# Attention scores from a key matrix folded per head, and three value tiles of sixteen in fp32

## The chip, the cores and the metric

The kernel runs on one NeuronCore of a Trainium2 chip, as one launch. Its five engines are TensorE (PE; its weight loads are listed as PEld), VectorE (DVE), ScalarE (ACT), GpSimd (POOL) and SyncE (SP, which here only issues DMAs). The metric is the device time in microseconds (us); lower is better.

## The reference

One transformer block with adaptive layer norm, on x of shape (4, 1024, 256), fp32:

```python
h = layernorm(x) * (1 + ca) + sa
c_q = h @ W_DQ + b_DQ; c_kv = h @ W_DKV + b_DKV            # 32 features each
q_c, k_c, v_c = up-projections of c_q / c_kv, 8 heads x 128
q_r = c_q @ W_QR + b_QR (8 heads x 32); k_r = h @ W_KR + b_KR (32, shared by all heads)
attn = softmax(concat(q_c, q_r) @ concat(k_c, k_r).T / sqrt(160)) @ v_c
x = x + ga * (attn @ W_O + b_O)
h = layernorm(x) * (1 + cb) + sb
x = x + gb * mixture_of_8_experts(h)      # top 1, capacity 768, GELU
```

The change is in the attention: 4 batches x 8 heads = 32 heads, each with a 1024 x 1024 score matrix.

## The kernel before

The program has four stages, each an `nc.Block`. Stage one normalises x, projects it to a key/value latent and a query latent of 32 features each, and folds the weights. Stage two is the attention, from about 86 to 605 us. Stage three projects, normalises again and routes. Stage four runs the experts. No engine crosses a block's end before the others have reached it.

In the attention no head's keys are ever expanded. A score is a product of a *folded query* with the batch's 64 key features (32 latent, 32 rotary), because W_UQ and W_UK are multiplied together in stage one (side product `GQS`, lines 575 and 397 to 409) into `GQ`, 98 rows by 8 heads by 128. fp32 precision is kept by splitting numbers into a high and a low fp16 part; row groups of 32 or 64 partitions hold the parts.

Names: `KA` [128, 4096] holds the key features (rows 0 to 63 high, 64 to 127 low), `KB` [65, 4096] the high part again with a row of -1, `KC` a copy of the high part for the second 512 keys on partitions 64 to 127, `CQ` [98, 4096] the query latents (high, low, high and two rows of 1), `QA` and `QB` a ring of three heads of folded queries, `prob` the exponentials in fp32 (8 tiles of 128 keys by 1024 queries), `prob_top` the upper 16 bits of `prob` read as bf16 in place, `prob_lo` the fp16 remainder, `VV` the values as two 32-column halves and a column of ones.

The order on each engine is written out by hand over slots (p, k), with p a head and k one of its 8 tiles of 128 keys. In slot (p, k):

- PE runs two score halves of tile k + 4 (line 710), each as two accumulating products of 512 queries, `KA` by `QA` (line 722) and `KB` by `QB` (line 723); a row of `QB` holds the query's row maximum, which the row of -1 subtracts. The two halves alternate between the PSUM banks `st_ps`, so each waits until ACT has read the same bank two halves before.
- PE runs `maxima` of head p + 2 (line 725): for 128 queries, two products of 64 rows each with the two halves of the keys (lines 732, 733), into the three banks `x_ps`. DVE reduces each bank to one column (line 859), and after 16 of them reduces those to `mz` (line 866).
- In slots 4 and 6 PE makes half of the folded query of head p + 3 (`query`, line 751) in `side_ps`; ACT copies its high part to `QA` (line 803), DVE subtracts to get the low part in `QB` (line 871). The next half waits for that.
- In slot 1 PE turns `mz` into 8 rows (line 758), ACT copies them (line 809), SP sends them by DMA into row 64 of `QB` (line 704).
- PE runs `values(p, k)` (line 771): 8 groups of 128 queries, each with `prob_top` and `prob_lo` as stationary operand and 65 columns of `VV` as moving one, 16 products in all.
- ACT makes the exponentials of tile k + 4 (line 799), two of 512 columns per slot.
- The subtraction `prob - prob_top` into `prob_lo` is POOL's (line 834), except for tile 5 of every head and tile 7 of odd heads, which `by_vector` gives to DVE (line 876): 6.5 of 8 tiles on POOL, 1.5 on DVE.
- At a head's end ACT copies the accumulators (line 816), DVE adds the halves (line 884) and inverts the sums (line 885), POOL normalises (line 841). `values(p + 1, 0)` waits for the first two.

Of the kernel before, what the change touches and what calls it, by code (L numbers as in the profile page):

```python
# [15 lines left out]
P = 128  # L16
# [22 lines left out]
QRING = 3  # L39


def adaln_block(nc, h_t, W_DQ, b_DQ, W_UQ, b_UQ, W_DKV, b_DKV, W_UK, b_UK, W_UV, b_UV, W_QR, b_QR,
# [20 lines left out]
    with ctx:  # L63
# [44 lines left out]
        KC = sb(inner, "KC", [P, B, HALF], fp16)  # L108
        KB = sb(inner, "KB", [LR + 1, N], fp16)
        CQ = sb(inner, "CQ", [QROWS, N], fp16)  # L110
        VV = sb(inner, "VV", [P, NT, VP], fp16)
        GQ = sb(inner, "GQ", [QROWS, H, P], fp16)
        mz = sb(inner, "mz", [P, ST], fp16)
        mrow = sb(inner, "mrow", [ST, 2, P], fp16)
# [28 lines left out]
        G = sb(one, "G", [QROWS, H, P])  # L143
# [52 lines left out]
        SHIFT, COLUMNS, GATES, UQ, UKV, PROJ, BIAS, GQS, SIDE = 0, 1, 2, 4, 6, 7, 9, 10, 11  # L196
        GATE_STEPS = 5

        with nc.Block() as block:
# [43 lines left out]
            def _(ac):  # L243
# [47 lines left out]
                for b in range(B):  # L291
# [5 lines left out]
                    nc.scalar.activation(KC[LR:P, b, :], k_ps[LR:P, HALF:S], ACT.Identity, bias=bk[LR:P, :]).then_inc(hi_done, 1)  # L297
# [6 lines left out]
                    nc.scalar.activation(CQ[0:3 * DC, b * S:(b + 1) * S], q_ps[0:3 * DC, :], ACT.Identity,  # L304
# [5 lines left out]
            def _(pool):  # L310
# [30 lines left out]
                fill(12, KB[LR:LR + 1, :], -1.0)  # L341
# [3 lines left out]
                fill(13, CQ[3 * DC:QROWS, :], 1.0)  # L345
                pool.wait_ge(const_p, 14)
                for g in range(2, NG):
                    power(g)

            @block.vector  # L350
            def _(v):
# [22 lines left out]
                def side_out(n):  # L374
# [15 lines left out]
                    elif n == UKV:  # L390
                        nc.vector.tensor_copy(ukvT[:], bank[:].rearrange("p (h c) -> p h c", h=H)).then_inc(side_done, 1)
                    elif n < BIAS:
                        nc.vector.tensor_copy(proj[:, n - PROJ, :], bank[:, 0:D]).then_inc(side_done, 1)
                    elif n == BIAS:
                        nc.vector.tensor_copy(attn_bias[:], bank[:, 0:D]).then_inc(side_done, 1)
                    else:
                        g_ps = bank[0:QROWS, 0:H * DC].rearrange("p (h c) -> p h c", h=H)
                        nc.vector.tensor_scalar(G[:, :, 0:DC], g_ps, SCALE, None, ALU.mult).then_inc(prep, 1)
                        nc.vector.tensor_scalar(G[:, :, LR:LR + DC], g_ps, SCALE, None, ALU.mult).then_inc(side_done, 1)
                        for r in range(2):  # L400
                            nc.vector.tensor_scalar(G[:, :, r * LR + DC:(r + 1) * LR], qr[:], SCALE, None, ALU.mult).then_inc(prep, 1)
                        v.wait_ge(prep, 3)
                        v.wait_ge(side_done, GQS + 1)
                        nc.vector.tensor_copy(GQ[:], G[:]).then_inc(prep, 1)
                        v.wait_ge(prep, 4)

                        nc.vector.tensor_tensor(GQ[64:QROWS, :, :], G[64:QROWS, :, :], GQ[64:QROWS, :, :], ALU.subtract).then_inc(prep, 1)
                        v.wait_ge(prep, 5)
                        nc.vector.tensor_copy(GQ[96:97, :, :], G[96:97, :, :]).then_inc(prep, 1)
# [12 lines left out]
                def keys_low(b):  # L422
                    at = slice(b * S, (b + 1) * S)
                    v.wait_ge(hi_done, 3 * b + 2)
                    nc.vector.scalar_tensor_tensor(KA[LR:P, at], k_ps[LR:P, :], bk[LR:P, :], KA[LR:P, at],
                                                   ALU.add, ALU.subtract).then_inc(lo_done, 1)
                    nc.vector.tensor_copy(KB[0:LR, at], KA[0:LR, at])

                def queries_low(b):
                    at = slice(b * S, (b + 1) * S)  # L430
                    v.wait_ge(hi_done, 3 * b + 3)
                    nc.vector.scalar_tensor_tensor(CQ[DC:2 * DC, at], q_ps[DC:2 * DC, :], bq[DC:2 * DC, :],
                                                   CQ[DC:2 * DC, at], ALU.add, ALU.subtract).then_inc(lo_done, 1)

                def take_values(b):
                    v.wait_ge(v_ready, b + 1)
                    for low in range(2):
                        nc.vector.tensor_copy(VV[:, b * ST:(b + 1) * ST, (1 - low) * DC:(2 - low) * DC],
                                              v_ps[:, :, low * LR:low * LR + DC]).then_inc(v_done, 1)

# [58 lines left out]
                side_out(GQS)  # L499
# [9 lines left out]
            def _(te):  # L509
# [30 lines left out]
                def values(b):  # L540
                    te.wait_ge(lo_done, 2 * b + 1)
                    if b:
                        te.wait_ge(v_done, 2 * b)
# [4 lines left out]
                def side(n):  # L548
# [67 lines left out]
                side(GQS)  # L616
                turn(7)
                values(2)
# [9 lines left out]
        QA = sb(two, "QA", [P, QRING, S], fp16)  # L628
        QB = sb(two, "QB", [LR + 1, QRING, S], fp16)
# [15 lines left out]
        sub_vector = sem("sub_vector")  # L645
# [3 lines left out]
        q_ready = sem("q_ready")  # L649
        qa_done = sem("qa_done")  # L650
        ql_done = sem("ql_done")
        max_done = sem("max_done")
        mrow_ready = sem("mrow_ready")
        mrow_done = sem("mrow_done")
# [10 lines left out]
        QUERY_SLOTS = (4, 6)  # L665
        FIRST_MAX = 0
        ROW_SLOT = 1

        def by_vector(n):

            return (5, 7) if n % 2 else (5,)

        def by_pool(n):

            return [k for k in range(ST) if k not in by_vector(n)]

        pool_before = [sum(len(by_pool(m)) for m in range(n)) for n in range(HEADS)]
        vector_before = [sum(len(by_vector(m)) for m in range(n)) for n in range(HEADS)]
# [11 lines left out]
        def maxima_of(p, k):  # L690

            n, s = (p + 2, k - FIRST_MAX) if k >= FIRST_MAX else (p + 1, k - FIRST_MAX + ST)
            return n, (2 * s, 2 * s + 1)

# [4 lines left out]
        with nc.Block() as block:  # L699
            @block.sync  # L700
            def _(sp):
                for n in range(HEADS):
                    sp.wait_ge(mrow_done, n + 1)
                    sp.dma_start(QB[LR:LR + 1, n % QRING, :].rearrange("a (t q) -> a t q", q=P),
                                 mrow[:, n % 2, :]).then_inc(mrow_in[n % 2], 16)

            @block.tensor
            def _(te):
                mm = nc.tensor.matmul

                def scores(n, k, f):
# [4 lines left out]
                    if k == 0:  # L716
                        te.wait_ge(qa_done, 2 * n + f + 1)
                        te.wait_ge(ql_done, 2 * n + f + 1)
                        te.wait_ge(mrow_in[n % 2], 16 * (n // 2 + 1))
                    at = slice(b * S + k * P, b * S + (k + 1) * P)  # L720
                    half = slice(f * HALF, (f + 1) * HALF)
# [3 lines left out]
                def maxima(n, q):  # L725
                    b = n // H
                    i = n * 16 + 2 * q
                    if i >= 2:
                        te.wait_ge(smax_done, i - 1)
                    te.wait_ge(qa_done, 2 * n + q // 4 + 1)  # L730
                    at = slice(q * P, (q + 1) * P)
                    mm(x_ps[i % 3][:], QA[0:LR, n % QRING, at], KA[0:LR, b * S:b * S + HALF], start=True, stop=True)  # L732
                    mm(x_ps[(i + 1) % 3][:], QA[LR:P, n % QRING, at], KC[LR:P, b, :], start=True, stop=True).then_inc(smax_ready, 1)  # L733
# [814 lines left out]
```

## Time and profile before

| | |
|---|---|
| median of 3 runs | 1004.4 us (1001.28 to 1005.44) |
| the profiled execution | 1002.6 us, of which the span is 1000.9 us |
| PE, busy share of the span | 88% |
| VectorE | 71% |
| ScalarE | 59% |
| GpSimd | 66% |
| mean granted TensorE clock | 0.943 of 2.4 GHz |
| attention stage, from its first product to its last normalisation | 86.0 to 604.7 us |

A busy share on PE counts overlapping matmuls as they are displayed, so a PE shown as busy may still be waiting inside; the distance from one start to the next is what a matmul costs. The rows come further below, after the change.

### The profile page before, as it was taken

The numbers are of one execution on the slowest core, as the hardware profiler recorded it, in microseconds if no ns is written. First come the engines' busy times: TensorE is split into PE (matmuls) and PEld (weight loads), VectorE is DVE, ScalarE is ACT, GpSimd is POOL, SyncE is SP. The second block draws the span as 40 slices with busy tenths as digits, with TensorE's granted clock in tenths as the row PEclk, the third lists the DMA queues.
The fourth block names the chain that finished last, engine by engine and source line by source line (L and its number), as shares of the span: only waits on it lengthen the run. The fifth ranks groups of instructions, "written<-read, shape, count | busy, mean of one in ns | idle before, by whom it ended". The sixth has DMA issues, their size and how long they took to land. (4 is left out here: it accounts for less than half of the span.)

```text
span 1000.9 us, 21467 instructions
## 1 busy us (share of the span) xinstructions
PE 881.8 (88%) x8406; PEld 527.7 (53%) x8406; DVE 713.9 (71%) x1315; ACT 588.0 (59%) x1004; POOL 655.7 (66%) x437
## 2 busy tenths in 40 slices
PE   4893899999999999999999988962499999999995
PEld 1350244444444444444444547862266777677764
DVE  4768888888888888888898836872075666566643
ACT  3750577777777777777777663664265446544650
POOL 4200599999999999999999993698404524442452
PEclk9995799999999999999999998985599999999998
DMA  9910000000000000000000004259525434543110
GB/s 279 339 43 0 1 2 2 2 2 2 2 2 2 2 2 2 2 2 2 2 2 1 3 1 169 99 198 320 201 69 162 143 107 140 175 142 123 43 52 19
DMA packets 48166, 71.61 MB, mean 72 GB/s; under 512 B 7508, under 2 KB 40473, under 8 KB 47938
## 3 DMA queue, kind: packets, MB, share of 16 engines
q1 hardware_dynamic: 38114, 53.13, 16.1%
q0 software_dynamic: 7680, 16.87, 5.2%
q8 instruction: 68, 1.11, 0.5%
q10 hardware_dynamic: 2272, 0.24, 0.2%
q14 instruction: 32, 0.26, 0.1%
HBM read 46.76 MB, written 29.67 MB: 76 GB/s over the span
## 5 line engine op out<-in xcount | busy, mean ns | idle before, releaser
L834 POOL TENSOR_TENSOR prob_lo<-prob 128x1024 f16<-128x1024 f32 x208 | 437.3, 2130 | 95.0 <-ACT prob L799 94.9
L799 ACT ACTIVATE prob<-st_ps 128x512 f32<-128x512 f32 x512 | 301.4, 597 | 131.8 <-PE st_ps L723 129.5
L859 DVE TENSOR_REDUCE part_max<-x_ps 128x1 f32<-128x512 f32 x512 | 325.1, 678 | 66.7 <-PE x_ps L733 65.7
L722 PE MATMUL st_ps<-QA,KA 128*128 128x512 f16 x512 | 198.1, 387 | 0.5 <-ACT prob L799 0.5
L723 PE MATMUL st_ps<-QB,KB 65*128 65x512 f16 x512 | 196.4, 384 | 0.0
L771 PE MATMUL acc_ps<-VV,prob 128*128 128x65 f16 x2048 | 159.3, 194 | 3.9 <-POOL prob_lo L834 3.9
L771 PEld LDWEIGHTS acc_ps<-VV,prob 128*128 128x128 bf16 x2048 | 143.6, 98 | 33.4 <-POOL prob_lo L834 6.1
L771 PE MATMUL acc_ps<-VV,prob_lo 128*128 128x65 f16 x2048 | 158.7, 194 | 0.0
L771 PEld LDWEIGHTS acc_ps<-VV,prob_lo 128*128 128x128 f16 x2048 | 134.9, 98 | 29.9
L1340 POOL DMA_INDIRECT out<-yo,xb x48 | 47.7, 993 | 153.3 <-DVE yo L1447 151.1
L732 PE MATMUL x_ps<-KA,QA 64*128 64x512 f16 x256 | 102.2, 399 | 20.8 <-DVE part_max L859 20.7
L1370 ACT ACTIVATE act_f<-g_ps,cols 128x768 f32<-128x768 f32 x64 | 57.6, 900 | 104.3 <-PE g_ps L1493 104.3
L1418 DVE TENSOR_TENSOR act_l<-act_f,act_h 128x768 f16<-128x768 f32 x64 | 59.9, 955 | 71.9 <-ACT act_h L1378 71.9
L1508 PE MATMUL y_ps<-w2h,act_h 128*128 128x256 f16 x384 | 104.8, 273 | 4.2 <-DVE act_l L1418 4.2
L1508 PE MATMUL y_ps<-w2l,act_h 128*128 128x256 f16 x384 | 104.7, 273 | 0.0
L1508 PE MATMUL y_ps<-w2h,act_l 128*128 128x256 f16 x384 | 104.7, 273 | 0.0
L733 PE MATMUL x_ps<-KC,QA 64*128 64x512 f16 x256 | 102.2, 399 | 0.0
L732 PEld LDWEIGHTS x_ps<-KA,QA 64*128 64x128 f16 x256 | 23.8, 93 | 122.6 <-DVE part_max L859 120.5
L722 PEld LDWEIGHTS st_ps<-QA,KA 128*128 128x128 f16 x512 | 49.5, 97 | 60.0 <-issue 36.5
L1333 POOL DMA_INDIRECT tb<-tbuf,xb x48 | 63.9, 1331 | 17.9 <-issue 14.3
L876 DVE TENSOR_TENSOR prob_lo<-prob 128x1024 f16<-128x1024 f32 x48 | 61.2, 1274 | 6.2 <-ACT prob L799 6.2
L1493 PE MATMUL g_ps<-xh,w1h 128*128 128x384 f16 x256 | 53.0, 330 | 1.8 <-DVE xl L1412 1.4
(177 smaller groups left out, 1346.7 us busy)
## 6 DMA issues: line engine op xcount, KB each, us to landing
w1f<-in_L_ffn_w SPq DMA_DIRECT2D x8, 1024.0 KB, 6.1
w2f<-in_L_ffn_w SPq DMA_DIRECT2D x8, 1024.0 KB, 6.1
xbuf<-zeros SPq DMA_DIRECT2D x7, 910.0 KB, 16.7
xb<-xbuf SPq DMA_DIRECT2D x8, 780.0 KB, 5.4
x<-in_L_attn_h_t SPq DMA_DIRECT2D x8, 512.0 KB, 8.9
out<-x SPq DMA_DIRECT2D x4, 1024.0 KB, 5.9
tbuf<-x SPq DMA_DIRECT2D x4, 1024.0 KB, 9.7
tbuf<-gb_row SPq DMA_DIRECT2D x4, 1024.0 KB, 4.7
```

Of the source, the lines that this page charges most:

```text
L722: mm(st_ps[i % 2][:], KA[:, at], QA[:, n % QRING, half], start=True, stop=False)
L723: mm(st_ps[i % 2][:], KB[:, at], QB[:, n % QRING, half], start=False, stop=True).then_inc(scores_ready, 1)
L732: mm(x_ps[i % 3][:], QA[0:LR, n % QRING, at], KA[0:LR, b * S:b * S + HALF], start=True, stop=True)
L733: mm(x_ps[(i + 1) % 3][:], QA[LR:P, n % QRING, at], KC[LR:P, b, :], start=True, stop=True).then_inc(smax_ready, 1)
L771: last = mm(acc_ps[:, q, 0:VC], part[:, k, q * P:(q + 1) * P], VV[:, b * ST + k, 0:VC], start=k == 0 and q % 4 == 0 and i == 0, stop=k == ...
L799: nc.scalar.activation(prob[:, k, f * HALF:(f + 1) * HALF], st_ps[i % 2][:], ACT.Exp).then_inc(exp_done, 1)
L834: nc.gpsimd.tensor_tensor(prob_lo[:, k, :], prob[:, k, :], prob_top[:, k, :], ALU.subtract).then_inc(sub_pool, 1)
L859: nc.vector.tensor_reduce(part_max[:, n % 2, item // 2, item % 2:item % 2 + 1], x_ps[i % 3][:], AX.X, ALU.max).then_inc(smax_done, 1)
L876: nc.vector.tensor_tensor(prob_lo[:, k, :], prob[:, k, :], prob_top[:, k, :], ALU.subtract).then_inc(sub_vector, 1)
L1333: nc.gpsimd.indirect_dma_start(out=tb[:, s, :], out_offset=None, in_=tbuf, in_offset=bass.IndirectOffsetOnAxis(ap=who(e, s), axis=0), boun ...
L1418: V.tensor_tensor(act_l[:, f, :], act_f[:, i % 3, :], act_h[:, f, :], ALU.subtract).then_inc(act_low, 1)
L1508: last = mm(y_ps[s % 2][:, 0:D], x[:, f, s * P:(s + 1) * P], w[:, u, f, :], start=c == 0 and f == 0, stop=c == 2 and f == FT - 1)
```

## The change

The fold is moved from the query side to the key side. Stage one now makes a matrix of shape [128 key features, 8 heads, 98], split into `GH` (high) and `GL` (low), in two side products `FOLD` and `FOLD + 1` of 16 small fp32 matrix products each, in place of one `GQS` of 8. In the attention, PE multiplies it with `KA` to get a head's *key features* in query-latent space, `KX` (rows 0 to 95 and one bias row 96 and 97, plus row 98, which stays -1), in a ring of four heads: two accumulating products for each half of 512 keys, in slots 1 and 3, three heads ahead. ACT copies them to fp16, DVE subtracts rows 64 to 96 to get a low part.

- A score half is then a single product of 99 rows: `KX` as stationary, `CQ` as moving operand. `CQ` has two copies, for even and odd heads, whose row 98 holds the row maxima. The second copy is made by one DMA of 98 x 8 KB at the start of the stage, for which head 1's maxima wait.
- The maxima are two products of 98 rows for each 128 queries, one per bank, each with its own semaphore count and wait. Their stationary operand is `queries_of`: every eighth column of `CQ`, a step of 16 bytes. Query 8g + j is thus on partition g for group j, so `mz` [128, 8] already has the order in which a row of `CQ` needs it, and SP sends it by a DMA with 128 runs of 16 bytes as soon as DVE has it. The turn by PE and the copy by ACT go.
- Tiles 1 and 6 of even heads and tile 3 of odd heads (`whole`) have no `prob_lo`. Their value products take `prob` itself in fp32 and `V32`, 33 columns in fp32: 8 fp32 products in place of 16 of 16 bits. POOL subtracts the other 6.5 tiles per head, DVE none.
- Stage one loses the copies `KC` (ACT) and the copy of `KA` to `KB` (DVE) and gains a DVE addition for `V32` per batch and a POOL fill.

```diff
@@ stage one: the fold
-        g_ps = bank[0:QROWS, 0:H * DC].rearrange("p (h c) -> p h c", h=H)
-        nc.vector.tensor_scalar(G[:, :, 0:DC], g_ps, SCALE, None, ALU.mult).then_inc(prep, 1)
...
+        nc.vector.tensor_scalar(G[:, heads, :], bank[:].rearrange("p (h c) -> p h c", h=4)[:, :, 0:QROWS],
+                                SCALE, None, ALU.mult).then_inc(side_done, 1)
+        v.wait_ge(side_done, n + 1)
+        nc.vector.tensor_copy(GH[:, heads, :], G[:, heads, :]).then_inc(prep, 1)
+        v.wait_ge(prep, i + 1)
+        nc.vector.tensor_tensor(GL[:, heads, :], G[:, heads, :], GH[:, heads, :], ALU.subtract)
...
-                    elif n == GQS:
-                        for h in range(H):
-                            last = mm(bank[0:QROWS, h * DC:(h + 1) * DC], uqT[:, h, 0:QROWS], ukvT[:, h, 0:DC], start=True, stop=True)
+                    elif n >= FOLD:
+                        for i in range(4):
...
+                            for r in (0, LR):
+                                mm(bank[r:r + DC, at], ukvT[:, h, 0:DC], uqT[:, h, 0:QROWS], start=True, stop=True)
+                                last = mm(bank[r + DC:r + LR, at], qr[:, h, :], ident[0:QROWS, 0:QROWS], start=True, stop=True)
...
-                side(GQS)
+                side(FOLD)
                 turn(7)
+                side(FOLD + 1)
@@ attention: which tiles
-        def by_vector(n):
-
-            return (5, 7) if n % 2 else (5,)
+        def whole(n):
+
+            return (3,) if n % 2 else (1, 6)
@@ attention, SP
+                sp.dma_start(CQ[0:QROWS, 1, :], CQ[0:QROWS, 0, :]).then_inc(copied, 16)
                 for n in range(HEADS):
-                    sp.wait_ge(mrow_done, n + 1)
...
+                    sp.wait_ge(max_done, n + 1)
+                    if n >= 2:
+                        sp.wait_ge(scores_ready, 2 * ST * (n - 1))
+                    sp.dma_start(CQ[QROWS:QROWS + 1, n % 2, b * S:(b + 1) * S].rearrange("a (g t) -> a g t", t=ST),
+                                 mz[:, n % 2, :]).then_inc(mrow_in[n % 2], 16)
@@ attention, PE
-                    mm(st_ps[i % 2][:], KA[:, at], QA[:, n % QRING, half], start=True, stop=False)
-                    mm(st_ps[i % 2][:], KB[:, at], QB[:, n % QRING, half], start=False, stop=True).then_inc(scores_ready, 1)
+                    mm(st_ps[i % 2][:], KX[:, n % KRING, k * P:(k + 1) * P],
+                       CQ[:, n % 2, b * S + f * HALF:b * S + (f + 1) * HALF], start=True, stop=True).then_inc(scores_ready, 1)
...
+                def maxima(n, j, f):
                     b = n // H
...
+                    if i >= 3:
+                        te.wait_ge(smax_done, i - 2)
+                    if j == 0 and f == 0:
+                        te.wait_ge(kl_done, 2 * n + 2)
...
+                    mm(x_ps[i % 3][:], queries_of[:, n % 2, b * P:(b + 1) * P, j],
+                       KX[0:QROWS, n % KRING, f * HALF:(f + 1) * HALF], start=True, stop=True).then_inc(smax_ready, 1)
...
+                def keys(n, f):
                     b, h = n // H, n % H
...
+                    if 2 * n + f:
+                        te.wait_ge(kl_done, 2 * n + f)
+                    at = slice(b * S + f * HALF, b * S + (f + 1) * HALF)
+                    mm(side_ps[0:QROWS, :], GH[:, h, :], KA[:, at], start=True, stop=False)
+                    mm(side_ps[0:QROWS, :], GL[:, h, :], KA[:, at], start=False, stop=True).then_inc(k_ready, 1)
...
+                    if k in whole(n):
+                        te.wait_ge(exp_done, (n * ST + k) * 2 + 2)
+                        for q in range(ST):
+                            last = mm(acc_ps[:, q, DC:VC], prob[:, k, q * P:(q + 1) * P], V32[:, b * ST + k, :],
+                                      start=False, stop=False)
...
                         if f == 0 and k == ST - 1 and is_head(p):
                             values(p, k)
...
+                        if is_head(p + 2):
+                            maxima(p + 2, k, f)
+                    if k in KEY_SLOTS and is_head(p + 3):
+                        keys(p + 3, KEY_SLOTS.index(k))
```

## Rows read from the trace of the kernel before

**Rows 1.** The page: its span, and busy time and share of each engine.
```profile
span 1000.9 us, 21467 instructions
...
PE 881.8 (88%) x8406; PEld 527.7 (53%) x8406; DVE 713.9 (71%) x1315; ACT 588.0 (59%) x1004; POOL 655.7 (66%) x437
```
**Rows 2.** Stretches: length, busy time per engine (instructions), granted clock, DMA share, GB/s.
```profile
80.00:110.00 30.00, 13.57 (x40) 2.65 (x40) 24.73 (x38) 5.65 (x10) 0.64 (x1) 0.50 0.00 0
...
400.00:500.00 100.00, 97.45 (x1176) 48.91 (x1173) 85.40 (x146) 71.74 (x131) 93.25 (x50) 1.00 0.01 2
```
**Rows 3.** Waits, 200 to 500 us: engine, line, whom; total, times, longest.
```profile
PEld x_ps L732 <- DVE part_max L859: 67.2, 136, 0.9
...
PEld side_ps L751 <- DVE QB L871: 6.4, 20, 0.5
```
**Rows 4.** Line 866, once per head: durations ns, first and last start.
```profile
L866 DVE TENSOR_REDUCE mz<-part_max x32: 169/170/172, 101.4 to 578.0; 128x8 f16<-128x16 f32 x32
```
**Rows 5.** Tile prob_lo, 200 to 500 us: count, duration min/median/max in ns.
```profile
L834 POOL TENSOR_TENSOR prob_lo<-prob x128: 1884/1888/2963, 198.5 to 499.7; 128x1024 f16<-128x1024 f32 x128
L876 DVE TENSOR_TENSOR prob_lo<-prob x29: 1212/1215/1217, 202.1 to 491.2; 128x1024 f16<-128x1024 f32 x29
```
**Rows 6.** Timeline of POOL, 409 to 417 us: start, length, engine, line, count, [idle before].
```profile
409.13 3.74 POOL L834 TENSOR_TENSOR prob_lo<-prob 128x1024 f16<-128x1024 f32 x2
...
414.12 2.96 POOL L834 TENSOR_TENSOR prob_lo<-prob 128x1024 f16<-128x1024 f32 x1 [0.68 <-ACT prob L799]
```
**Rows 7.** Timeline of PE over one slot of a head.
```profile
404.50 0.39 PE L732 MATMUL x_ps<-KA,QA 64*128 64x512 f16 x1
...
404.82 0.39 PE L722 MATMUL st_ps<-QA,KA 128*128 128x512 f16 x1
405.05 0.38 PE L723 MATMUL st_ps<-QB,KB 65*128 65x512 f16 x1
405.26 0.38 PE L751 MATMUL side_ps<-CQ,GQ 98*128 98x512 f16 x1
405.48 0.19 PE L771 MATMUL acc_ps<-VV,prob 128*128 128x65 f16 x1
...
405.97 0.38 PE L722 MATMUL st_ps<-QA,KA 128*128 128x512 f16 x1
```
**Rows 8.** Timelines of PE in stage three: fp32 products, back to back.
```profile
641.73 0.51 PE L1227 MATMUL lp_ps<-cols,hsT 128*128 128x8 f32 x4
642.09 0.42 PE L1218 MATMUL tr_ps<-ident,hs 128*128 128x128 f32 x2
642.35 0.38 PE L1202 MATMUL oT_ps<-ident,o_n 128*128 128x128 f32 x2
```
**Rows 9.** Timelines of ACT and DVE: instructions back to back.
```profile
423.43 1.08 ACT L799 ACTIVATE prob<-st_ps 128x512 f32<-128x512 f32 x2 [0.47 <-PE st_ps L723]
...
415.25 1.91 DVE L859 TENSOR_REDUCE part_max<-x_ps 128x1 f32<-128x512 f32 x3
```
**Rows 10.** Timelines of DVE and PE, end of stage one.
```profile
62.51 0.42 DVE L427 COPY KB<-KA 64x1024 f16<-64x1024 f16 x1
...
67.53 0.42 DVE L398 TENSOR_SCALAR G<-t_ps 98x256 f32<-98x256 f32 x1
...
71.55 0.49 DVE L438 COPY VV<-v_ps 128x256 f16<-128x256 f16 x2
...
63.44 1.49 PE L575 MATMUL t_ps<-ukvT,uqT 128*98 128x32 f32 x16
```
**Rows 11.** Timeline of DVE, start of the attention stage.
```profile
89.87 8.27 DVE L859 TENSOR_REDUCE part_max<-x_ps 128x1 f32<-128x512 f32 x12
```
**Rows 12.** Timeline of POOL, the last two heads.
```profile
583.58 14.96 POOL L834 TENSOR_TENSOR prob_lo<-prob 128x1024 f16<-128x1024 f32 x7
```
**Rows 13.** DMA issues: destination, queue, count, KB each, median us to landing.
```profile
xbuf<-zeros SPq DMA_DIRECT2D x7, 910.0 KB, 16.7
...
b2w<-in_L_ffn_b SPq DMA_DIRECT2D x8, 128.0 KB, 3.3
```

More of the change, by code:

```diff
@@ L142, in adaln_block @@
         ukvT = sb(one, "ukvT", [P, H, 2 * DC])
-        G = sb(one, "G", [QROWS, H, P])
+        G = sb(one, "G", [P, H, QROWS])
         zeros = sb(one, "zeros", [P, 7, ROW])
@@ L192, in adaln_block @@
         biased = sem("biased")
-        SHIFT, COLUMNS, GATES, UQ, UKV, PROJ, BIAS, GQS, SIDE = 0, 1, 2, 4, 6, 7, 9, 10, 11
+        SHIFT, COLUMNS, GATES, UQ, UKV, PROJ, BIAS, FOLD, SIDE = 0, 1, 2, 4, 6, 7, 9, 10, 12
         GATE_STEPS = 5
@@ L340, in _ @@
                 pool.wait_ge(ln_rstd, 1)
-                fill(12, KB[LR:LR + 1, :], -1.0)
+                fill(12, KX[3 * DC:QROWS + 1, :, :], -1.0)
                 pool.wait_ge(const_p, 13)
@@ L344, in _ @@
                 pool.wait_ge(ln_rstd, 2)
-                fill(13, CQ[3 * DC:QROWS, :], 1.0)
+                fill(13, CQ[3 * DC:QROWS, 0, :], 1.0)
                 pool.wait_ge(const_p, 14)
-                for g in range(2, NG):
+                power(2)
+                pool.wait_ge(ln_rstd, 3)
+                fill(14, V32[:, :, DC:DC + 1], 1.0)
+                pool.wait_ge(const_p, 15)
+                for g in range(3, NG):
                     power(g)
@@ L396, in side_out @@
                     else:
-                        g_ps = bank[0:QROWS, 0:H * DC].rearrange("p (h c) -> p h c", h=H)
-                        nc.vector.tensor_scalar(G[:, :, 0:DC], g_ps, SCALE, None, ALU.mult).then_inc(prep, 1)
[L399 to L409, printed above, removed]
+                        i = n - FOLD
+                        heads = slice(4 * i, 4 * i + 4)
+                        nc.vector.tensor_scalar(G[:, heads, :], bank[:].rearrange("p (h c) -> p h c", h=4)[:, :, 0:QROWS],
[4 more added lines that the diff above has]
+                        nc.vector.tensor_tensor(GL[:, heads, :], G[:, heads, :], GH[:, heads, :], ALU.subtract)
                 def bound_gates():
@@ L498, in _ @@
                 queries_low(2)
-                side_out(GQS)
+                side_out(FOLD)
+                side_out(FOLD + 1)
                 take_values(2)
@@ L663, in adaln_block @@
         AHEAD = 4
-        QUERY_SLOTS = (4, 6)
-        FIRST_MAX = 0
-        ROW_SLOT = 1
-        def by_vector(n):
-            return (5, 7) if n % 2 else (5,)
+        KEY_SLOTS = (1, 3)
+        queries_of = CQ[0:QROWS, :, :].rearrange("c r (g t) -> c r g t", t=ST)
+        def whole(n):
+            return (3,) if n % 2 else (1, 6)
         def by_pool(n):
-            return [k for k in range(ST) if k not in by_vector(n)]
+            return [k for k in range(ST) if k not in whole(n)]
         pool_before = [sum(len(by_pool(m)) for m in range(n)) for n in range(HEADS)]
-        vector_before = [sum(len(by_vector(m)) for m in range(n)) for n in range(HEADS)]
         def slots():
```

171 lines of the change are left out of this document (58 added, 113 removed).

## Prediction

> **What bounds the kernel now.** I read the page first [rows 1]: PE is busy 88% of the span, but no engine bounds all four stages. The table of stretches [rows 2] says where: from 400 to 500 us PE shows 97%, GpSimd 93%, VectorE 85%, ScalarE 72%, at the full granted clock (1.00, the level of 2.4 GHz). Such a stretch repeats for 32 heads. One instruction per head dates them [rows 4]: 476.6 us from the first to the last of 32, so 15.4 us per head. Everything of weight lies in this number.
>
> Who sets it? The distance between starts on PE over one slot [rows 7] gives prices: a two-product score half 0.44, one product of 512 columns 0.215 (0.43 for two), a pair of maxima products 0.32, one tile of 16 value products 0.49. A head takes 16 x 0.44 + 8 x 0.32 + 2 x 0.215 + 8 x 0.49 + 0.15 for the maxima's turn = 14.1 us. PE thus waits some 1.3 us per head, mostly for VectorE's maxima [rows 3]. GpSimd: a subtraction takes 1.888 us at the median and 2.963 at most [rows 5]; back to back two take 3.74, 1.85 each [rows 6]. The long ones are those beside VectorE's own subtraction of 1.215 (414.12 us is one): 1.07 us extra, 1.5 times per head. GpSimd needs 6.5 x 1.85 + 1.5 x 1.07 + 0.6 (normalisation) = 14.2 of 15.4 us. VectorE: reductions follow each other by 0.61, exponentials by 0.49 [rows 9]. So PE and GpSimd are both near the bound and hold each other up. A change gains only if it relieves both, and this one does.
>
> **The change part by part, on PE.** Scores: one product for each half, 16 x 0.215 = 3.44 in place of 7.04. Maxima: 16 products that each fill 98 rows, so no two run side by side: 3.44 in place of 2.56. Keys: 4 x 0.215 = 0.86 in place of 0.43. The turn of maxima (0.15) goes. Values: 6.5 tiles x 0.49 = 3.19 in place of 3.92. New are 1.5 fp32 tiles of 8 logical products per head. In stage three an fp32 product of few columns is recorded as two instructions, four starting within 0.36 us [rows 8], 0.09 each; where the moving operand has 128 columns they are 0.13 apart (two in 0.26, 642.09 to 642.35). The weight load is what they have in common, and 33 columns are nearer to 8 than to 128: I take 0.11, 16 x 0.11 = 1.76 per tile, 2.64 per head (2.2 to 3.1 by the two rows). Sum: 3.44 + 3.44 + 0.86 + 3.19 + 2.64 = 13.6 us.
>
> **GpSimd, VectorE, ScalarE.** GpSimd keeps 6.5 tiles, at 1.85 as VectorE no longer subtracts beside it: 12.0 + 0.6 = 12.6. VectorE loses 1.5 x 1.2: 16 x 0.61 + 2 key halves at 0.6 + 0.7 at the head's end = 11.7. ScalarE: 18 x 0.49 + 0.4 = 9.2. PE is the bound alone. An fp32 tile occupies PE long and GpSimd not at all, so GpSimd catches up there; the longest run of other tiles is five (4 to 7 of an odd head, then 0): 5 x 1.85 + 0.6 = 9.9 against about 7 on PE, covered by the lead of four slots in which exponentials stand ahead of values.
>
> **Waits that stay or come on PE.** (a) The second key half waits until VectorE has subtracted the first, behind that slot's two reductions; now the like wait costs 6.4 us in 20 [rows 3], 0.3 each; PE then holds back that slot's values and the next scores. (b) Slots shrink to 4 x 0.215 + 0.49 = 1.35 us. The score banks are still two, and a bank comes free about 1.05 us after its product starts; between the last slot and the next head's first, where the values are done early, the second bank returns after only 0.86: 0.2. (c) At the head's end VectorE has 0.4 of adding and 0.2 of the row reduction between two maxima: the third bank is late once, 0.2. Together 0.7, and 13.6 + 0.7 = 14.3 us per head. For the waits I keep 0.3 (only the first) to 1.4 (as now), for the period 13.5 to 15.4.
>
> **What costs nothing, and what hides it.** The maxima's DMA is issued by SP once VectorE is through with slot 7 and needed by the first score half of slot 4 on: some 6 us of PE work. The nearest row for 128 partitions is `b2w` with 3.3 us to landing [rows 13]; beyond 6 us every further microsecond is added to each head, behind it all of PE's queue. SP's new wait on scores of the head before last is long met, and only row DMAs queue behind it. VectorE's new wait for the row DMA of two heads ago, and the fp32 tile's wait for exponentials alone, are older than those they replace. The copy of `CQ` (0.8 MB) is issued at 86 us and needed when head 0's maxima are through, 14 us later; the row nearest in size landed in 16.7 us, one of seven issued together [rows 13], so 0 to 3 us, and I take 0.
>
> **Stage one.** Its end is VectorE's queue. `GQS` occupies it from 67.53 to 71.55 [rows 10], 4.0 us; two `FOLD`s take three operations on 392 columns each, about 1.4 us by the 256-column row of 0.42 and more for the two on SBUF: 2.8. Two copies to `KB` go (2 x 0.34), two additions for `V32` come (2 x 0.4). But `FOLD + 1` may use the bank only when `FOLD` has been read, and PE then needs 32 instructions; 16 took 1.33 us [rows 10], 98 rows by 32 columns turned round, so 2.7: VectorE waits some 2 us. Net +0.9 (-0.7 if PE is early, +3 if the later latents are late).
>
> **Start and end of the attention.** PE runs at half the clock there (0.50 from 80 to 110 us [rows 2]), the level of 1.2 GHz, after a stretch without work. Head 0's maxima now wait for both key halves and their low parts: +2.2 us. Then 12 reductions took 8.27 us in pairs with a wait in each [rows 11], 0.69 apiece; with a count per bank they follow by 0.61: -1.3 per head over two heads, so nothing in sum until the first score, and -1 up to the first values since the score has one product fewer (+-2 for both). At the end the maxima are done and GpSimd alone sets the pace: its last seven subtractions in a row took 14.96 us [rows 12], 2.1 each, where 1.85 would make 13.0; over 10.5 tiles and the slower normalisation -4 (-1 to -6). Stages three and four are untouched: 0.
>
> **Sum.** 30 heads run all kinds of work: 30 x (15.4 - 14.3) = -33. With +0.9, -1 and -4: -37. The profiled execution took 1002.6 us (span 1000.9 and 1.7 around it), 1.8 below the median of 1004.4: 1002.6 - 37 = 966.
>
> **A rule that speaks against it.** The stationary operand of the maxima takes every eighth fp16 column, a step of 16 bytes; the largest step in the rows is prob_top's 4 bytes, inside the 0.49 of a value tile [rows 7].
>
> The Trainium skill, SBUF — State Buffer, section Door 1: The DMA port swizzle, says that SBUF is read in lines of 16 bytes and each access that crosses to a new line pays a penalty. By it each of the 16 loads per head is slower, and no run here shows by how much; that is the second rival's story.
>
> **The rivals.** 1: *GpSimd or lockstep stays the bound.* PE's waits for maxima and banks do not shrink, or GpSimd's long subtractions have another cause than VectorE and stay at their mean of 2.14 us (6.5 x 2.14 + 0.6 = 14.5, with waits 15.0). Period 15.0: -12 + 0.9 - 1 - 2 = 988. For it: PE already waits 1.3 now. Against: the duration has two values, and the long ones coincide with VectorE's. 2: *the maxima's loads are not hidden.* A load lies under the product before it, 0.215 us. If it outlasts that by 0.1 (the excess of a pair of maxima now, 0.32 over 0.215), 16 x 0.1 x 30 = +48: 1014, slower. It decides from 0.07. Against: the load would have to take several times what a contiguous one can take in a value tile of 0.49 / 16 = 0.03. 3: *fp32 products are dearer.* If a load and a product of the 16 in a tile don't overlap, 0.11 + 0.09 = 0.20 each: 1.5 x 16 x 0.09 x 30 = +65: 1031, slower; it decides from 0.155. Against: rows 8, where they do overlap. 4: *the change does more*: waits shrink to 0.3 and fp32 comes at 0.09: period 13.4, about 940.
>
> **How the numbers follow.** Forecast 966: 0.62, with its own range of 952 to 980. Rival 1: 0.18; rival 2: 0.05; rival 3: 0.05; rival 4: 0.10. What a measurement of this kernel can tell from no change is about 0.5%, 5 us. Faster: 0.62 + 0.10 + most of rival 1 = 0.87; same 0.04; slower 0.09. The range, 945 to 998, leaves out the two slower rivals and the end of the fourth.
>
> **What would show it.** Row 866 14.3 us apart; line 834 at 1.89 us throughout; fp32 products near 0.11 us apart; maxima 0.215 from their neighbours (rival 2: 0.3); PE's largest waits at the second key half; the stage's first score still near 106 us. It is wrong if PE waits long for the row DMA, if GpSimd has no gaps, or if the granted clock falls inside the heads, where PE's own instructions would cost double.

## The result and the profile after

The changed kernel takes 975.7 us at the median of 4 runs (974.99 to 976.06), against 1004.9 us for the kernel before in the same rounds: a ratio of 0.9716, 95% interval 0.9691 to 0.974. That is 29 us where the forecast had 37 (966 us); the range of 945 to 998 holds it. The profiled execution took 975.4 us.

The page of the changed kernel, in the order of [rows 1]:

```profile
span 973.7 us, 20139 instructions
...
PE 865.9 (89%) x7974; PEld 605.8 (62%) x7974; DVE 670.3 (69%) x1266; ACT 563.6 (58%) x968; POOL 607.0 (62%) x438
```

Its stretches, as in [rows 2] (length, busy time of PE, PEld, DVE, ACT, POOL, granted clock, DMA share, GB/s):

```profile
80.00:110.00 30.00, 20.99 (x42) 5.96 (x43) 23.34 (x36) 6.02 (x10) 0.20 (x1) 0.50 0.09 27
...
400.00:500.00 100.00, 97.21 (x1114) 67.55 (x1114) 82.42 (x145) 69.98 (x131) 87.07 (x52) 1.00 0.01 2
```

GpSimd's 93 us in that stretch are now 87, while PE shows the same 97 as before: it is the engine without gaps. The row reduction of each head in the changed kernel (answering [rows 4]):

```profile
L840 DVE TENSOR_REDUCE mz<-part_max x32: 169/170/171, 100.7 to 555.2; 128x8 f16<-128x16 f32 x32
```

GpSimd's subtraction there (answering [rows 5]):

```profile
L809 POOL TENSOR_TENSOR prob_lo<-prob x134: 1892/1895/1903, 198.4 to 498.9; 128x1024 f16<-128x1024 f32 x134
```

Its waits from 200 to 500 us (answering [rows 3]: engine, line, whom it waited for; total, times, longest):

```profile
POOL prob_lo L809 <- ACT prob L781: 40.0, 52, 1.4
PEld x_ps L730 <- DVE part_max L833: 19.7, 42, 0.6
...
PEld side_ps L738 <- DVE KX L845: 15.2, 20, 0.8
...
PEld st_ps L718 <- ACT prob L781: 10.1, 21, 0.5
```

From the first to the last head's row reduction there are 31 periods in 454.5 us: 14.66 us each, where [rows 4] gives 15.37. The 27.2 us between the spans divide so: 0.7 before the first of these reductions (100.7 against 101.4 us), 22.1 in the 31 periods, 2.9 from the last of them to the end of the attention (23.8 us; before 26.7), the other 1.5 in the stages behind. GpSimd's subtraction has one duration, 1.895 us, where it had 1.888 with a tail at 2.963: the long ones went with VectorE's subtraction. GpSimd now waits for exponentials, and these wait for PE's score products.

Two places where PE waits, in its timeline of the changed kernel (start, length): the second key half, and the second score bank at a head's turn. Neighbours are 0.22 apart when nothing is waited for.

```profile
415.07 0.38 PE L730 MATMUL x_ps<-KX,CQ 98*128 98x512 f16 x1
415.76 0.42 PE L738 MATMUL side_ps<-KA,GH 128*98 128x512 f16 x1 [0.31 <-DVE KX L845]
416.02 0.38 PE L739 MATMUL side_ps<-KA,GL 128*98 128x512 f16 x1
...
423.52 0.38 PE L718 MATMUL st_ps<-CQ,KX 99*128 99x512 f16 x1
423.74 0.38 PE L730 MATMUL x_ps<-KX,CQ 98*128 98x512 f16 x1
424.15 0.39 PE L718 MATMUL st_ps<-CQ,KX 99*128 99x512 f16 x1
```

The key half starts 0.69 after the product ahead of it, 0.47 more than the work needs; the score half 0.41 after, 0.19 more. One fp32 tile in the same view:

```profile
400.93 1.87 PE L749 MATMUL acc_ps<-V,prob 128*128 128x33 f32 x16
402.63 0.38 PE L718 MATMUL st_ps<-CQ,KX 99*128 99x512 f16 x1
```

From 400.93 to 402.63 it holds PE for 1.70 us.

### The profile page after: what moved, and what is told of

The parts are those of the page before. It is cut to its first block and busy times, and to the rows that moved or that the text cites. A ratio compares the mean times of both kernels' runs of the same rounds, so it can differ in the third digit from the quotient of the medians.

```text
span 973.7 us, 20139 instructions
## 1 busy us (share of the span) xinstructions
PE 865.9 (89%) x7974; PEld 605.8 (62%) x7974; DVE 670.3 (69%) x1266; ACT 563.6 (58%) x968; POOL 607.0 (62%) x438
## 3 DMA queue, kind: packets, MB, share of 16 engines
q1 hardware_dynamic: 42322, 53.93, 16.8%
## 5 line engine op out<-in xcount | busy, mean ns | idle before, releaser
L809 POOL TENSOR_TENSOR prob_lo<-prob 128x1024 f16<-128x1024 f32 x208 | 390.4, 1896 | 120.4 <-ACT prob L781 119.9
L730 PE MATMUL x_ps<-KX,CQ 98*128 98x512 f16 x512 | 205.0, 405 | 4.0 <-DVE KX L845 1.4
L718 PE MATMUL st_ps<-CQ,KX 99*128 99x512 f16 x512 | 197.2, 386 | 2.8 <-ACT prob L781 1.5
L756 PE MATMUL acc_ps<-VV,prob 128*128 128x65 f16 x1664 | 128.5, 193 | 2.9 <-POOL prob_lo L809 2.9
L756 PE MATMUL acc_ps<-VV,prob_lo 128*128 128x65 f16 x1664 | 128.1, 193 | 0.0
L730 PEld LDWEIGHTS x_ps<-KX,CQ 98*128 98x128 f16 x512 | 73.9, 145 | 64.0 <-DVE part_max L833 37.1
L749 PEld LDWEIGHTS acc_ps<-V,prob 128*128 128x128 f32 x768 | 94.2, 193 | 4.0
L749 PE MATMUL acc_ps<-V,prob 128*128 128x33 f32 x768 | 89.7, 272 | 0.0
L718 PEld LDWEIGHTS st_ps<-CQ,KX 99*128 99x128 f16 x512 | 54.8, 107 | 37.0 <-ACT prob L781 22.2
L1297 POOL DMA_INDIRECT tb<-tbuf,xb x48 | 63.9, 1332 | 17.0 <-issue 14.3
L785 ACT ACTIVATE KX<-side_ps 98x512 f16<-98x512 f32 x64 | 38.2, 597 | 51.0 <-PE side_ps L739 51.0
```

Source lines behind the costliest of these rows:

```text
L718: mm(st_ps[i % 2][:], KX[:, n % KRING, k * P:(k + 1) * P], CQ[:, n % 2, b * S + f * HALF:b * S + (f + 1) * HALF], start=True, stop=True).t ...
L730: mm(x_ps[i % 3][:], queries_of[:, n % 2, b * P:(b + 1) * P, j], KX[0:QROWS, n % KRING, f * HALF:(f + 1) * HALF], start=True, stop=True).t ...
L749: last = mm(acc_ps[:, q, DC:VC], prob[:, k, q * P:(q + 1) * P], V32[:, b * ST + k, :], start=False, stop=False)
L756: last = mm(acc_ps[:, q, 0:VC], part[:, k, q * P:(q + 1) * P], VV[:, b * ST + k, 0:VC], start=k == 0 and q % 4 == 0 and i == 0, stop=k == ...
L809: nc.gpsimd.tensor_tensor(prob_lo[:, k, :], prob[:, k, :], prob_top[:, k, :], ALU.subtract).then_inc(sub_pool, 1)
L1297: nc.gpsimd.indirect_dma_start(out=tb[:, s, :], out_offset=None, in_=tbuf, in_offset=bass.IndirectOffsetOnAxis(ap=who(e, s), axis=0), boun ...
```

## The experiments

Theory: in the changed kernel PE alone sets the heads' period, with 13.6 us of its own work and 1.0 of waits, and both parts of the change were needed, the single score product for PE and the fp32 tiles for GpSimd and VectorE. Rivals: the relief of GpSimd is the whole gain; the maxima's strided loads or the lockstep of the engines have taken what is missing. All ratios are to the kernel before, run on the same chip. The period is read as above, from the first to the last row reduction over 31.

### fp32 tiles alone, in the kernel before

```diff
-            return (5, 7) if n % 2 else (5,)
+            return (3,) if n % 2 else (1, 6)
...
                     if k in by_vector(n):
+                        te.wait_ge(exp_done, (n * ST + k) * 2 + 2)
+                        for q in range(ST):
+                            last = mm(acc_ps[:, q, DC:VC], prob[:, k, q * P:(q + 1) * P], V32[:, b * ST + k, :], start=False, stop=False)
```

> The kernel before with one part of the change alone: tiles 1 and 6 of even heads and tile 3 of odd heads take the fp32 value products, and VectorE subtracts no tile. Theory (TensorE sets the heads' period, and the fp32 products are a price, not a gain): a fp32 tile costs 1.70 us in the changed kernel against 0.49, so TensorE's own work goes from 14.1 to 15.9 us per head; with a wait of 0.7 to 1.3 the period is 16.6 to 17.2, about 1035 to 1055 us, slower. Line 834 falls to 1.89 us throughout. Rival (the relief of GpSimd is where the gain comes from): period at or under 15.0, at most 993 us.

Measured: 1057.5 us, ratio 1.0552 (1.0524 to 1.0581), period 17.16 us. Slower by 55 us, somewhat beyond the theory's range. GpSimd's subtraction was 1.892 us throughout, so it had its relief and the kernel lost all the same. The relief is not the gain; PE pays for fp32 and needs the score product's 3.6 us first.

### The fp32 tiles undone

```diff
-            return (3,) if n % 2 else (1, 6)
+            return (5, 7) if n % 2 else (5,)
...
+                    if is_head(ns) and ks in whole(ns):
+                        subtract(ns, ks)
```

> The changed kernel with one part undone: all value tiles take 16-bit products again, and VectorE subtracts tile 5 of each head and tile 7 of odd heads as in the kernel before. Theory (both parts are needed: with TensorE's own work at 11.8 us GpSimd and VectorE take over): GpSimd needs 6.5 x 1.85 + 1.5 x 1.07 + 0.6 = 14.2 us per head; VectorE 11.7 + 1.8 = 13.5; with some waiting the period is 14.3 to 15.0, 965 to 985 us, about as the changed kernel; the longest subtraction on GpSimd is 2.96 us again. Rival (TensorE alone matters): period near 13, about 930 us.

Measured: 1070.7 us, ratio 1.0706 (1.0654 to 1.0757), period 17.53. Both expectations fell, the theory's by 85 us. (The added subtraction stands in VectorE's slot ahead of the key half's low part.) The timelines of VectorE, GpSimd and PE in this kernel show how:

```profile
401.32 2.71 DVE L847 TENSOR_TENSOR prob_lo<-prob 128x1024 f16<-128x1024 f32 x1
404.06 0.69 DVE L843 TENSOR_TENSOR KX<-side_ps,KX 33x512 f16<-33x512 f32 x1
...
401.06 4.73 POOL L807 TENSOR_TENSOR prob_lo<-prob 128x1024 f16<-128x1024 f32 x2 [0.23 <-ACT prob L779]
...
401.49 0.38 PE L732 MATMUL x_ps<-KX,CQ 98*128 98x512 f16 x1
404.81 0.42 PE L740 MATMUL side_ps<-KA,GH 128*98 128x512 f16 x1 [2.94 <-DVE KX L843]
...
406.60 0.63 PE L732 MATMUL x_ps<-KX,CQ 98*128 98x512 f16 x1
```

GpSimd's subtraction began at 401.06, VectorE's at 401.32, and VectorE's was through only at 404.03, 2.71 us instead of the 1.215 of [rows 5]. Behind it in VectorE's queue stood the key half's low part, behind that PE's key product, behind that everything PE had. The last row, a product displayed at 0.63 in place of 0.38, is PE at half the clock just after: in the 100 us from 200 on the granted clock was 0.88.

The Trainium skill, SBUF — State Buffer, section SBUF: two separate sides, says that the port pair which VectorE and GpSimd share is an exclusive lock held for a whole instruction: whichever begins first keeps it and the other blocks. The rows agree in both directions: 1.215 us on VectorE and 2.96 on GpSimd in the kernel before (both begin at 414.12), the reverse here, where 1.6 of GpSimd's 1.9 us were still to run and 1.6 + 1.2 makes 2.8 (2.71 measured).

### The same, VectorE's subtraction in other slots

```diff
-            return (5, 7) if n % 2 else (5,)
+            return (0, 1) if n % 2 else (1,)
```

> As the run without fp32 products (1070.7 us), but VectorE subtracts tile 1 of even heads and tiles 0 and 1 of odd ones, so its subtraction falls into slots 5 and 6, no longer right ahead of the key halves' low parts in slots 2 and 4. In that run VectorE's subtraction took 2.66 us at the median as it waited for GpSimd's, the key half behind it came 3.3 us late, and TensorE's granted clock fell. Theory (this collision, not the missing fp32 tiles, made the 95 us): with it gone GpSimd at 14.2 us per head is the bound, period 14.3 to 15.0, 965 to 990 us. Rival (VectorE's and GpSimd's subtractions cost as much wherever they stand): over 1030 us.

Measured: 1017.6 us, ratio 1.013 (1.0113 to 1.0148), period 15.95. Moving the subtraction away from the key half gives back 53 us, but the theory's 965 to 990 was missed again. VectorE's subtraction took 1.72 us at the median. What it stood in front of now, in the timelines of VectorE and PE:

```profile
416.83 1.72 DVE L847 TENSOR_TENSOR prob_lo<-prob 128x1024 f16<-128x1024 f32 x1
418.47 0.68 DVE L831 TENSOR_REDUCE part_max<-x_ps 128x1 f32<-128x512 f32 x1
...
417.24 0.38 PE L720 MATMUL st_ps<-CQ,KX 99*128 99x512 f16 x1
419.20 0.44 PE L732 MATMUL x_ps<-KX,CQ 98*128 98x512 f16 x1 [1.58 <-DVE part_max L831]
```

PE waits 1.7 us beyond its pitch for a maxima bank. With slots of 1.35 us, three banks are a buffer of one and a half slots, and a subtraction of 1.7 in VectorE's queue exhausts it. Adding GpSimd's needs to a sum says nothing of this.

The queue is not the whole loss. The granted clock, 1.00 inside the heads of the changed kernel, is 0.93 here:

```profile
200.00:500.00 300.00, 261.57 (x3095) 156.19 (x3093) 270.54 (x423) 196.65 (x359) 264.47 (x142) 0.93 0.01 2
```

With its two levels, 0.93 costs PE at most 0.07 of the period, 1.1 us per head (an estimate, as if PE worked all the time at the lower level). Right behind the wait shown, from 421 to 423 us, the clock is 0.50. That the waits bring it down is suggested by this order in time; no run separates the two.

### VectorE's subtraction left out of the kernel before

```diff
-                        te.wait_ge(sub_vector, vector_before[n] + by_vector(n).index(k) + 1)
+                        te.wait_ge(exp_done, (n * ST + k) * 2 + 2)
...
+                            stationary = flat_lo[:, q * P:(q + 1) * P] if i and k in by_vector(n) else part[:, k, q * P:(q + 1) * P]
```

> The kernel before with VectorE's 48 subtractions left out: for these tiles the low product reads a constant tile of zeros, so the attention output lacks their low part and is not the reference's. All products of TensorE stay, 14.1 us of them per head; GpSimd falls from 14.2 to 12.6 us, VectorE by 1.8. Theory (TensorE was within its waits the bound before): the period falls by part of the 1.3 us of waits, to 14.6 to 15.1, so 980 to 995 us. Rival (GpSimd was hardly holding anything): no change, over 1000 us. If it falls to 14.2 or less (970 us) the relief alone would have done what the whole change did.

Measured: 996.4 us, ratio 0.9943 (0.9919 to 0.9968), period 15.27. Between the theory and the rival, just over the upper end of what the theory gave: with every subtraction by VectorE gone and GpSimd at 1.89 us throughout, the kernel before gains 6 us, 8 at most. Its waits for maxima sum to 67.7 us from 200 to 500 us, where [rows 3] has 67.2. PE's 14.1 us and these waits were its bound; GpSimd, though near it in the sum, held up very little.

### fp32 products priced

The whole tiles get two 16-bit products, the low one with a constant tile, and nobody subtracts for them:

```diff
+                            stationary = flat_lo[:, q * P:(q + 1) * P] if i and k in whole(n) else part[:, k, q * P:(q + 1) * P]
```

> The changed kernel, where the three of sixteen value tiles take 16-bit products whose low part is a constant tile of zeros, in place of fp32 products; nobody subtracts for them. It leaves out these tiles' low part, so its output is not the reference's. It shows what the fp32 products cost: TensorE's own work falls from 13.6 to 11.8 us per head, GpSimd stays at 12.9. Theory (TensorE is the bound of the changed kernel and GpSimd stands close behind): period 12.9 to 13.4, about 925 to 940 us. Rival (TensorE is not the bound): over 960 us.

Measured: 922.2 us, ratio 0.9189 (0.9171 to 0.9207), period 12.89. PE's own work is less by 1.5 x 1.21 = 1.8 us and the period fell by 1.77. The stretch from 400 to 500 us:

```profile
400.00:500.00 100.00, 96.92 (x1303) 62.44 (x1301) 93.69 (x164) 79.87 (x148) 98.58 (x59) 1.00 0.01 2
```

GpSimd now shows 98.6%, 12.7 us per head, where the prediction has 12.6 and the theory here 12.9: it is the next bound. The period could thus hardly have fallen further, and that it fell by PE's saving within 0.1 us doesn't prove that price alone; the 1.70 us in the timeline does. Against the run with VectorE's subtraction in other slots, whose products are as cheap, this one lacks chiefly VectorE's 48 subtractions (the tiles stand elsewhere too). The two lie 95 us apart, 2 us for each, the lower granted clock included (1.00 here, 0.93 there: by the estimate above up to 33 of the 95 us). In the kernel before the same 48 were worth 6.

### Key slots

```diff
-        KEY_SLOTS = (1, 3)
+        KEY_SLOTS = (1, 5)
```

> The changed kernel with the second key half made in slot 5 in place of slot 3, so that VectorE has four slots for the first half's low part. In the changed kernel TensorE waits for it about 0.45 us per head. Theory (TensorE is the bound, so a wait taken away is gained): 30 x 0.45 = 13 us less, about 962 us. Rival (lockstep: the wait only moves to the score or maxima banks): under 4 us less, 972 us or more.

Measured: 959.7 us, ratio 0.9583 (0.9558 to 0.9608), period 14.11. The theory's 13 us became 16 by the medians (13 by the ratios): PE's wait for the key half is gone from its list, and the period fell by 0.55. This wait of PE was paid in full.

### Permuted queries

```diff
+                for b in range(B):
+                    nc.gpsimd.tensor_copy(CP[:, b * S:(b + 1) * S].rearrange("c (t g) -> c t g", g=P),
+                                          CQ[0:QROWS, 0, b * S:(b + 1) * S].rearrange("c (g t) -> c t g", t=ST)).then_inc(turned_queries, 1)
...
-                    mm(x_ps[i % 3][:], queries_of[:, n % 2, b * P:(b + 1) * P, j],
+                    mm(x_ps[i % 3][:], CP[:, b * S + j * P:b * S + (j + 1) * P],
```

> The changed kernel with a second copy of the query latents in the order of the maxima, made once by GpSimd before its first subtraction, so that the maxima's stationary operand has a step of 2 bytes in place of 16. The weight loads of the maxima are shown at 0.145 us in the changed kernel, those of the scores at 0.107. Theory (the slower load lies under a product of 0.22 us and shows only where TensorE has just waited): loads fall to 0.10, the period by 0 to 0.2 us, 969 to 976 us. Rival (the step of 16 bytes costs at each of the 16 products, 0.03 to 0.05): period down by 0.5 to 0.8, 950 to 960 us.

Measured: 972.6 us, ratio 0.9685 (0.9669 to 0.9701), period 14.53. The loads of the maxima's operand, in the groups by form from 200 to 500 us (busy, mean ns of one), first of the changed kernel, then of this one:

```profile
L730 PEld LDWEIGHTS x_ps<-KX,CQ 98*128 98x128 f16 x327 | 47.0, 144 | 34.4 <-DVE part_max L833 19.7
```
```profile
L733 PEld LDWEIGHTS x_ps<-KX,CP 98*128 98x128 f16 x330 | 32.3, 98 | 34.4 <-DVE part_max L840 19.4
```

144 ns become 98, and the kernel gains 3 us, 0.1 per head (the intervals of the two ratios overlap; the periods differ by 0.13). The step costs 46 ns a load, and most of it is hidden under the product of 0.22 before it. By the rule of 16-byte lines (the Trainium skill, SBUF — State Buffer, section Door 1: The DMA port swizzle) a load with a step of 16 bytes pays; the trace agrees. The prediction's second rival is answered: its mechanism exists, at a price of 0.1 us per head and not 1.6.

### The order at a head's end

```diff
-                        if f == 0 and k == ST - 1 and is_head(p):
+                        if f == 1 and k == ST - 1 and is_head(p):
                             values(p, k)
```

The same for ScalarE's copy of the accumulators; with the key slots 1 and 5.

> The changed kernel with the second key half in slot 5 (959.7 us by itself) and the last value tile of a head between the second score half and the second maxima product of slot 7, with ScalarE's copy of the accumulators behind both exponentials. TensorE waits 0.2 us per head there for the second score bank. Theory (TensorE is the bound, each wait of it is paid in full): 6 us less than with the key slots alone, about 954 us. Rival (the accumulators' chain, now later, takes its place): 959 us or more.

Measured: 960.4 us, ratio 0.956 (0.9543 to 0.9578), period 14.16, against 959.7 and 14.11 for the key slots alone: nothing, as the rival forecast. PE's longest waits in this kernel, 200 to 500 us, no longer name the score bank, where the key slots alone have 9.9 us. But the accumulators' sum stands at 7.3, where it was 5.0, and that of the maxima banks at 21.4, where it was 16.8. So the wait moved, and more to the maxima banks than to the rival's accumulators:

```profile
PEld x_ps L730 <- DVE part_max L833: 21.4, 42, 0.6
...
PEld acc_ps L756 <- DVE both L852: 7.3, 21, 0.4
DVE both L852 <- ACT raw L793: 6.0, 11, 0.5
```

### Fewer fp32 tiles, and a faster kernel

```diff
         KEY_SLOTS = (1, 5)
-            return (3,) if n % 2 else (1, 6)
+            return (3,)
```

> Key slots 1 and 5 (959.7 us by itself, 14.1 us per head) and one fp32 tile per head, tile 3, in place of one and a half. TensorE's own work falls by 0.5 x 1.21 to 13.0 us per head, GpSimd's rises by 0.5 x 1.85 to 13.6. Theory (TensorE is the bound, GpSimd is 1 us behind it, so the best share of fp32 tiles lies where the two meet): period 13.7 to 14.0, 946 to 957 us. Rival (GpSimd's queue, with seven tiles in a row, holds TensorE up): 960 us or more.

Measured: 943.8 us, ratio 0.941 (0.9379 to 0.9441), period 13.59. From 200 to 500 us (columns as for the stretches):

```profile
200.00:500.00 300.00, 295.99 (x3610) 204.84 (x3609) 267.85 (x463) 225.78 (x418) 298.73 (x177) 1.00 0.01 2
```

GpSimd is busy for 298.7 of 300 us: it is the bound now. The period fell by 0.52, where half a tile is 0.6 of PE's work, and ended somewhat below the theory's 13.7.

The other three combine this with the permuted copy:

> Key slots 1 and 5 and the second copy of the query latents in the order of the maxima (3 us by itself). If the two are independent, 956 to 958 us; if the slow loads showed only beside the wait that the key slots remove, 959 to 960 us.

> All three: key slots 1 and 5, the permuted copy, one fp32 tile per head. TensorE 13.0 us and GpSimd 13.6 us per head. Where GpSimd is the bound the permuted copy brings nothing: the same time as without it, within 1 us. Where TensorE is still the bound, 3 us less.

> Key slots 1 and 5, the permuted copy, and five fp32 tiles in four heads (two in one head, one in the others). TensorE 13.3, GpSimd 13.1 us per head: they meet. Theory (each bound is a straight line in the share of fp32 tiles): about 0.2 to 0.3 us per head under either neighbour, 945 to 952 us. Rival (irregular heads cost waits of their own): no better than one tile per head.

| kernel (all with key slots 1 and 5) | fp32 tiles per head | us | ratio (interval) | period |
|---|---|---|---|---|
| key slots | 1.5 | 959.7 | 0.9583 (0.9558 to 0.9608) | 14.11 |
| + permuted | 1.5 | 956.8 | 0.9545 (0.9507 to 0.9582) | 14.02 |
| + permuted | 1.25 | 950.8 | 0.9477 (0.9447 to 0.9507) | 13.77 |
| + permuted | 1 | 942.5 | 0.9389 (0.9358 to 0.942) | 13.52 |
| not permuted | 1 | 943.8 | 0.941 (0.9379 to 0.9441) | 13.59 |

With the key slots the permuted copy brings 2.9 us and 0.09 of the period, as it did without them, so the two look independent; at one tile, where GpSimd is full, it is worth 1.4 us. Both differences lie inside the intervals. From 1.5 tiles to 1 the period falls by 0.25 for each quarter tile, where PE's 1.21 a tile would give 0.30. At one tile GpSimd's need is 7 x 1.85 + 0.6 = 13.55 and it is busy for 299.9 of 300 us: PE's line has met GpSimd's there. At 1.25 tiles GpSimd still has 15.8 us of waits in 300, so PE bounds, and the theory's hope of a period under both neighbours fell; its range of time held. The rival, that irregular heads cost waits of their own, was right that this kernel would be no better than one tile per head. The other explanation, that the two lines meet nearer to one tile than was expected, gives the same order, and the run doesn't decide between them.

One fp32 tile per head with key slots 1 and 5 takes 62 us off the kernel before.

## Why the prediction was right, and where it was off

- **Direction and the new bound: right.** It said that PE and GpSimd had to be relieved together. Relieving GpSimd alone gave 6 us, or a loss of 55 with fp32 tiles; relieving PE and leaving VectorE's subtraction in place gave a loss of 13 or of 68 us. It said that PE would bound alone: GpSimd's waits, the key slots and the cheap products show it.
- **Why both were needed: only in part as it said.** It saw PE and GpSimd holding each other up at 14.1 and 14.2 us. But with GpSimd at 12.6 us and PE's products unchanged the period only went from 15.37 to 15.27, so GpSimd was not a second bound of that kernel. What made VectorE's subtractions unbearable was what stood behind them in VectorE's queue once PE's slots were shorter, and the prediction had no term for that.
- **PE's own work: right, 13.6 us.** A product of 512 columns was 0.22 apart (0.215 taken, +0.15 per head), the fp32 tile 1.70 us (1.76 taken, -0.1). The third rival is gone: the weight loads of fp32 do overlap.
- **PE's waits: the step that was mis-sized.** 0.7 us forecast; 14.66 - 13.6 = 1.05 measured, which over 30 heads is the 10 us between forecast and result. Wait (a), the second key half, was taken at 0.3 from today's row and is 0.47 in the timeline, 0.55 by the run that removes it: slots had become shorter, while VectorE's two reductions and its subtraction, which the wait spans, had not. Wait (b), the score bank, was 0.2 as forecast, but was worth nothing when removed. Wait (c), the maxima bank, stands at 19.7 us in 42 waits in the list, but the work beside it is counted in; how much of it is pure wait stays open.
- **GpSimd at 1.85 us apart throughout: right**, and so the part of rival 1 on GpSimd fell. Its other part, that PE's waits don't shrink, came half true: 1.3 us became 1.05, and the period of 14.66 lies midway between the forecast's 14.3 and the rival's 15.0.
- **Stage one: wrong sign.** +0.9 us forecast, -3.0 measured: VectorE's last operation there ends at 82.66 and not at 85.67. The wait for `FOLD + 1` did not come, and without it the prediction's own durations give -1.1 (not the -0.7 in its bracket), which is what VectorE saved from its addition to `KA` on (59.28 to 82.66 us, where it took 61.19 to 85.67). The other 1.9 us had been gained before that addition started: it waits for ScalarE, which no longer makes a copy to `KC` first (0.68 us each; 0.9 of the 1.9 are there at the batch before, where the addition starts at 44.36 and not at 45.24). The prediction put these copies at nothing. The 32 recorded fp32 instructions of one `FOLD` (16 products), put at 2.7 us by the 16 of [rows 10], started four together, as the timeline of PE in the changed kernel shows:

```profile
62.33 0.27 PE L580 MATMUL t_ps<-uqT,ukvT 128*32 128x98 f32 x1
62.34 0.27 PE L581 MATMUL t_ps<-ident,qr 98*32 98x98 f32 x1
62.34 0.27 PE L580 MATMUL t_ps<-uqT,ukvT 128*32 128x98 f32 x1
62.35 0.27 PE L581 MATMUL t_ps<-ident,qr 98*32 98x98 f32 x1
62.44 0.25 PE L580 MATMUL t_ps<-uqT,ukvT 128*32 128x98 f32 x1
...
62.96 0.25 PE L581 MATMUL t_ps<-ident,qr 98*32 98x98 f32 x1
63.14 1.10 PE L523 MATMUL t_ps<-ident,xn 128*128 128x128 f32 x8
```

  All 32 started within 0.63 us, and what follows them 0.81 after the first. Their outputs lie on four different groups of 32 partitions, while each of the 16 before filled 98 partitions; the shapes differ too (98 columns by 32, in place of 32 by 98), and no run separates the two.
- **Start of the attention: 0 forecast, +3.4.** The first score product started at 106.5 us against 106.1, from a start 3 us earlier. VectorE's maxima were to follow at 0.61 us, but at half the clock (0.50 from 80 to 110 us) PE needs 0.43 for each and 0.86 for a key half, and waits for low parts in between:

```profile
102.86 2.06 PE L730 MATMUL x_ps<-KX,CQ 98*128 98x512 f16 x4
105.60 0.66 PE L738 MATMUL side_ps<-KA,GH 128*98 128x512 f16 x1 [0.67 <-DVE KX L845]
106.06 0.63 PE L739 MATMUL side_ps<-KA,GL 128*98 128x512 f16 x1
106.48 0.63 PE L718 MATMUL st_ps<-CQ,KX 99*128 99x512 f16 x1
```

  The errors at stage one and here cancel, by luck, to a first score 0.4 us later, where the sum had 0.9.
- **End of the attention: -4 forecast, -2.9 measured.** GpSimd's last subtractions run at 1.86 apart, but the last head gives it seven tiles where it gave six.
- **The maxima's DMA: hidden, right.** Its median time to landing is 1.9 us, for 128 runs of 16 bytes, against 3.3 taken from [rows 13]; nothing waits for it.

## What to carry to other kernels

Price a wait by the work that it spans on the other engine, not by its size today: a change that shortens the slots around it makes it longer, and a slot order that was harmless becomes the bound. Where VectorE and GpSimd both read two SBUF tensors, count each such operation at up to its own time plus the other's, and look at what stands behind it in the queue: the same 48 operations were worth 6 us in one schedule and about 95 in the next, where the granted clock fell too. And when work can be moved between two engines in small shares, try one share to each side of the planned one: here the best of those tried lay at one tile per head and not at one and a half.

## What was not expected of the hardware

- Four recorded fp32 instructions with outputs on different groups of 32 partitions start within 0.02 us of each other; 32 of them with 98 columns moving take 0.81 us, where 16 with 98 output partitions and 32 columns moving took 1.33.
- A stationary operand with a step of 16 bytes takes 144 ns to load by the trace, one of 2 bytes 98, and costs the kernel 3 us in 512 loads.
- VectorE's two-input subtraction takes 1.215 us or up to 2.97, by whether it or GpSimd's began first.
- In the run where PE stood idle for 3 us at VectorE's subtraction, the granted clock was 0.89 on average from 200 to 500 us, with products at the lower level right behind such a wait; with waits of 1.7 us in other slots it was 0.93; in the changed kernel, with waits of up to 0.8 us there, it was 1.00.
